# Attention in a two-layer network on one core: maxima placed by VectorE's room, and softmax denominators partly summed on GpSimd

## The reference

```python
q = x @ q_w.T ; k, v = split(x @ kv_w.T)          # 16 query heads, 4 key heads, head size 32
q, k = apply_rope(q), apply_rope(k)
logits = einsum('bhqd,bhkd->bhqk', q, k_ctx) / sqrt(32)
logits = logits + causal_mask
probs = softmax(logits, axis=-1)
out = einsum('bhqk,bhkd->bhqd', probs, v_ctx)
return out @ c_w.T
```

## Time and profile before

| | |
|---|---|
| runs (3) | median 1434.9 us, 1433.83 to 1436.38 |
| profiled execution | 1431.71 us, of which the span of the instructions is 1430.0 us |
| TensorE matmuls (PE) | busy 1348.8 us, 94% of the span |
| VectorE (DVE) | 973.9 us, 68% |
| ScalarE (ACT) | 661.3 us, 46% |
| GpSimd (POOL) | 698.8 us, 49% |
| mean granted clock of TensorE | 0.98 of full speed |
| chain that ended last | PE 65%, DVE 22%, ACT 5%, POOL 3% |

### The profile page before, as it was taken

One profiled execution on the slowest core, in us unless ns is written; L12 is line 12 of the kernel. 1 busy time (PEld: TensorE's weight loads), 2 busy tenths in 40 slices (PEclk: granted clock), 3 DMA queues, 4 the chain that ended last, 5 costly groups with the idle time before them and its releaser, 6 DMA issues.

```text
span 1430.0 us, 19458 instructions
## 1 busy us (share of the span) xinstructions
PE 1348.8 (94%) x7206; PEld 918.9 (64%) x7206; DVE 973.9 (68%) x1959; ACT 661.3 (46%) x1151; POOL 698.8 (49%) x836
## 2 busy tenths in 40 slices
PE   6988999999989899989999999999999999999996
PEld 5875445555455454555554447788888888888885
DVE  5997475755657776676665534577668767886776
ACT  6654233231314554445463574455454645454442
POOL 2676131421313323234243366487678768766863
PEclk9999999999999899999999999999999999999998
DMA  9100110203213111134020411522223232432300
GB/s 336 63 1 1 74 59 16 89 1 96 74 44 97 53 46 49 35 86 143 3 75 10 135 58 60 205 89 89 89 89 147 99 114 98 158 122 88 118 30 29
DMA packets 46270, 116.86 MB, mean 82 GB/s; under 512 B 3420, under 2 KB 4448, under 8 KB 42336
## 3 DMA queue, kind: packets, MB, share of 16 engines
q1 hardware_dynamic: 45104, 114.31, 23.8%
q10 hardware_dynamic: 1072, 1.31, 0.3%
HBM read 92.28 MB, written 23.07 MB: 81 GB/s over the span
## 4 chain that ended last, share of the span: by engine, by line
PE 65%; DVE 22%; ACT 5%; POOL 3%; issue 3%; DMA 1%; SPq 0%; POOLq 0%; DVEq 0%; ACTq 0%
PE PS L1657 63%; DVE cm L626 4%; DVE SM L642 3%; DVE PS L829 2%; DVE SM L638 2%; PE PS L1666 1%; DVE tm L626 1%; ACT EX L1241 1%; DVE hm L635 1%; DVE SM L643 1%; DMA rw<-in_L_ffn_w_up 1%; POOL xA L1472 1%; POOL SM L1472 1%; DVE SM L632 1%; DVE hm L626 1%
## 5 line engine op out<-in xcount | busy, mean ns | idle before, releaser
L1241 ACT ACTIVATE EX<-PS 128x512 f32<-128x512 f32 (+3 forms) x384 | 170.2, 495 | 154.9 <-PE PS L1657 153.9
L1472 POOL TENSOR_TENSOR ws_g<-rw,ws_g 128x512 fp32r<-128x512 f32 x64 | 138.5, 2164 | 124.8 <-ACT ws_g L1062 124.8
L1472 POOL TENSOR_TENSOR SM<-SM 128x1 f32<-128x1 f32 x128 | 82.5, 644 | 233.3 <-DVE SM L632 230.5
L1657 PE MATMUL PS<-KG,QG 96*128 96x512 f32 (+3 forms) x384 | 141.1, 392 | 21.5 <-DVE SM L829 9.0
L1576 POOL TENSOR_SCALAR_AFFINE_SELECT EX<-EX 128x128 f32<-128x128 f32 x256 | 75.3, 303 | 161.7 <-ACT EX L1241 158.3
L829 DVE CUSTOM_DVE_ANT_0 PS<-PS,MW 128x128 f32<-128x128 f32 (+3 forms) x256 | 122.4, 500 | 43.9 <-PE PS L1657 43.3
L1657 PE MATMUL PS<-QG,KG 98*128 98x512 f32 (+3 forms) x384 | 135.6, 382 | 3.2 <-ACT EX L1241 3.0
L1441 ACT ACTIVATE ab<-hm 128x512 f32<-128x512 f32 x64 | 40.5, 633 | 203.6 <-DVE hm L626 203.6
L1657 PE MATMUL PS<-ws_d,HH 128*128 128x512 f32 x528 | 125.7, 389 | 0.7 <-DVE HH L626 0.7
L638 DVE TENSOR_REDUCE SM<-PS 128x1 f32<-128x512 f32 x128 | 87.7, 686 | 55.4 <-PE PS L1657 55.1
L1657 PEld LDWEIGHTS PS<-QG,KG 98*128 98x128 f32 x384 | 72.0, 192 | 76.2 <-issue 45.3
(11 more groups left out here) (204 smaller groups left out, 2798.7 us busy)
## 6 DMA issues: line engine op xcount, KB each, us to landing
rw<-in_L_ffn_w_gate SPq DMA_DIRECT2D x16, 1024.0 KB, 5.1
rw<-in_L_ffn_w_up SPq DMA_DIRECT2D x16, 1024.0 KB, 5.1
rw<-in_L_ffn_w_down SPq DMA_DIRECT2D x16, 1024.0 KB, 6.9
QG<-qs SPq DMA_DIRECT2D x48, 256.0 KB, 4.5
raw<-in_L_ffn_w SPq DMA_DIRECT2D x3, 2816.0 KB, 11.7
qs<-stg SPq DMA_DIRECT2D x16, 512.0 KB, 3.5
xA<-xs SPq DMA_DIRECT2D x2, 2048.0 KB, 8.8
ys<-xA SPq DMA_DIRECT2D x4, 1024.0 KB, 5.9
```

The lines of the kernel that those rows point to most:

```text
L1241: e.activation(EX[:, n % 16, 0:W], PS[:, score_bank(n), 0:W], ACT.Exp, scale=ISQ, bias=0.0).then_inc(S["ex"], 1)
L1472: return e.tensor_tensor(out, a, b, op)
L1657: return e.matmul(out, l, r, start=start, stop=stop, skip_group_check=free)
```

## The change

Three things are changed.

1. **Places of the maxima.** From unit 144 on (group 3 and later), the steady rate of nine per ten chunks with its two bounds is replaced by `room[n]`, a number for what a chunk leaves to VectorE (more for wide scores, projections and units; less for statistics, rotations, the transposes of the denominators), and `effort(x)`, what a maximum takes. Each half of a group has a window of chunks, and its units are spread over it in proportion. The transposes `h` follow where 6000 of room have gone by. Within a chunk the other parts stand ahead of the maxima. With it, unit 10 goes from the chunks 126/130 to 114/118 and unit 11 from 154/158 to 174/178; the copies and subtractions of the output weights CW from 170-182 to 194-206; SP's write of unit 10 from 143 to 132, and its load of the residual rows from 200 to 206.

2. **Sums on GpSimd.** In groups 2 to 6, second half, the exponentials of steps j = 0 to 3 are added up per head into a new tile ES [128, 4, 512] (`add_up`: EX + EX for j = 1, then ES + EX), 12 additions for each group, 60 in all.

3. **Ones products.** For these four steps `weigh` multiplies by ones once, ES at j = 3, where it had multiplied EX at each. New waits: the ones product on the last addition, ScalarE's `exp` on the addition that reads the slot of the ring four steps back.

```diff
+        ES = at("ES", [128, 4, 512], F32, 24)
...
+        def added(t):
+
+            return 2 <= steps3[t][0] <= 6 and steps3[t][1] == 1 and steps3[t][2] < 4
+
+        def esum_at(t, a):
+
+            return 12 * (steps3[t][0] - 2) + 4 * max(0, steps3[t][2] - 1) + a + 1
...
-        for n, y in ((26, 8), (82, 9), (130, 10), (158, 11)):
+        for n, y in ((26, 8), (82, 9), (118, 10), (178, 11)):
...
+        room = []
+        for n in range(NS):
+            r = 120 + 3 * width(n // 4)
+            r += sum({"u": 1200, "V": 1200, "p": 1200, "t3": -600, "VT": 1024}.get(t[0], 0) for t in behind[n])
+            r -= 1700 * (n % 48 in (8, 24)) + 2400 * (n % 48 in (10, 27)) + 5000 * (n in rotate)
+            r -= 1600 * (n + 6 in proj_at) + 2600 * (n - 2 in proj_at) + 2600 * (n in (28, 30, 34, 36))
+            room.append(max(0, r))
...
+        def effort(x):
+            g, f, a, i, k0 = units[x]
+            return 1450 if k0 + 512 <= 128 * i else 300 + 10 * (128 * (i + 1) - k0) // 4
...
+        for x0, x1, n0, n1 in [(48 * g + 16 * f, 48 * g + 16 + 32 * f, max(98, 48 * g - 51 + 14 * f), 48 * g - 37 + 34 * f)
+                               for g in range(3, 8) for f in range(2)]:
+            total, seen, n = sum(effort(x) for x in range(x0, x1)), 0, n0
+            for x in range(x0, x1):
+                while sum(room[n0:n + 1]) * total < seen * sum(room[n0:n1]):
+                    n += 1
+                seen += effort(x)
+                behind[n].append(("m", x))
+            behind[later(n, 6000)].append(("h", x0 // 48 * 2 + x0 % 48 // 16))
...
             def exp(n):
...
+                if n >= 16 and added(n // 4 - 4):
+                    w.wait_ge(S["esum"], esum_at(n // 4 - 4, n % 4))
...
+            def add_up(n):
+
+                t, a = divmod(n, 4)
+                first = steps3[t][2] == 1
+                w.wait_ge(S["ex"], n + 1)
+                if first:
+
+                    w.wait_ge(S["pj"], 20)
+                    w.wait_ge(S["pvd"], t - 9 if t - 9 >= 12 * 2 else 0)
+                else:
+                    w.wait_ge(S["esum"], esum_at(t - 1, a))
+                tt(ES[:, a, :], EX[:, (n - 4) % 16, :] if first else ES[:, a, :], EX[:, n % 16, :], ALU.add).then_inc(
+                    S["esum"], 1)
...
+                if not added(t) or j == 3:
+                    first = 3 if added(t) else 0
+                    if j == first:
+                        w.wait_ge(S["de"], 2 * g + f)
+                    if added(t):
+                        w.wait_ge(S["esum"], esum_at(t, 3))
                     for a in range(4):
-                        last = mm(PS[32 * a:32 * a + 32, bank, q0 - 512 * f:512], left,
-                                  EX[:, (4 * t + a) % 16, 0:width(t)], j == 0, j == 4 * f + 3, free=True)
+                        last = mm(PS[32 * a:32 * a + 32, 7, q0 - 512 * f:512], onesf[:, 0:32],
+                                  ES[:, a, :] if added(t) else EX[:, (4 * t + a) % 16, 0:width(t)],
+                                  j == first, j == 4 * f + 3, free=True)
```

More of the change, by code:

```diff
@@ L45 @@
 pj ue rp qh ql d_w0 d_w1 d_k0 d_k1 d_k2 d_k3 d_q00 d_q01 d_q10 d_q11 vj vt vtp va
-sx mxr nm mtp mth mtl d_m0 d_m1 st ex sel pvd oe de rd oo d_xc cwh cwl
+sx mxr nm mtp mth mtl d_m0 d_m1 st ex sel pvd oe de rd oo esum d_xc cwh cwl
 ehi ot ep pc mv6 rs6 en ey d_ys0 d_ys1
@@ L330, in network, with later @@
             behind[n] += [("p", i, 0), ("p", i, 1)]
-        last = 12
-        for x in range(48, 8 * 48):
-            g, n = divmod(x, 48)
-            last = max(last, 12 + (x - 48) * 9 / 10, 48 * g - 36 + n - 16 if n >= 16 else 0)
-            behind[int(last)].append(("m", x))
-            if n in (15, 47):
-                behind[int(last) + 3].append(("h", 2 * g + n // 32))
+        room = []
[5 more added lines that the diff above has]
+            room.append(max(0, r))
+        def later(n, r):
+            m = n + 1
+            while sum(room[n + 1:m]) < r:
+                m += 1
+            return m
+        def effort(x):
+            g, f, a, i, k0 = units[x]
+            return 1450 if k0 + 512 <= 128 * i else 300 + 10 * (128 * (i + 1) - k0) // 4
+        for x in range(48, 144):
+            last = max(12 + (x - 48) * 9 // 10, x - 52 if x >= 112 else 0)
+            behind[last].append(("m", x))
+            if x % 48 in (15, 47):
+                behind[last + 3].append(("h", x // 48 * 2 + x % 48 // 32))
+        for x0, x1, n0, n1 in [(48 * g + 16 * f, 48 * g + 16 + 32 * f, max(98, 48 * g - 51 + 14 * f), 48 * g - 37 + 34 * f)
[7 more added lines that the diff above has]
+            behind[later(n, 6000)].append(("h", x0 // 48 * 2 + x0 % 48 // 16))
+        for n in range(NS):
+            parts, more = ([t for t in behind[n] if (t[0] == "m") == kind] for kind in (False, True))
+            behind[n] = []
+            for t in parts:
+                behind[n] += [t]
+            behind[n] += more
         tops = bits(first + [t for v in behind for t in v])
@@ L523, in sp_program @@
                         m_in(t[1])
-                if n in (42, 96, 143, 172):
-                    unit_out((42, 96, 143, 172).index(n) + 8)
+                if n in (42, 96, 132, 172):
+                    unit_out((42, 96, 132, 172).index(n) + 8)
                 if n in (100, 112, 156, 202):
@@ L530, in sp_program @@
                     k_in(4 + g)
-                if n == 200:
+                if n == 206:
                     written(10)
@@ L1309, in attention @@
                         drain(2 * (n // 48) - 1)
-                    if n in (170, 174, 178, 182):
-                        c = (n - 170) // 4
+                    if n in (194, 198, 202, 206):
+                        c = (n - 194) // 4
                         w.wait_ge(S["d_xs1"], 16)
@@ L1571, in attention @@
                         scale(2 * (n // 48))
+                    if added(n // 4) and steps3[n // 4][2] > 0:
+                        add_up(n)
                     if diagonal(n // 4):
@@ L1863, in weigh @@
                 w.wait_ge(S["va"], 3 if g < 4 else 4)
-                for bank, left, drained in ((6, VG[g // 4][:, j, g % 4 * 32:(g % 4 + 1) * 32], "oe"),
-                                            (7, onesf[:, 0:32], "de")):
-                    if j == 0:
-                        w.wait_ge(S[drained], 2 * g + f)
+                if j == 0:
+                    w.wait_ge(S["oe"], 2 * g + f)
+                for a in range(4):
+                    last = mm(PS[32 * a:32 * a + 32, 6, q0 - 512 * f:512], VG[g // 4][:, j, g % 4 * 32:(g % 4 + 1) * 32],
+                              EX[:, (4 * t + a) % 16, 0:width(t)], j == 0, j == 4 * f + 3, free=True)
+                if not added(t) or j == 3:
[4 more added lines that the diff above has]
+                        w.wait_ge(S["esum"], esum_at(t, 3))
                     for a in range(4):
-                        last = mm(PS[32 * a:32 * a + 32, bank, q0 - 512 * f:512], left,
-                                  EX[:, (4 * t + a) % 16, 0:width(t)], j == 0, j == 4 * f + 3, free=True)
+                        last = mm(PS[32 * a:32 * a + 32, 7, q0 - 512 * f:512], onesf[:, 0:32],
+                                  ES[:, a, :] if added(t) else EX[:, (4 * t + a) % 16, 0:width(t)],
+                                  j == first, j == 4 * f + 3, free=True)
                 last.then_inc(S["pvd"], 1)
```

## The result

The changed kernel takes 1444.6 us (median), the kernel before 1436.4 beside it: ratio 1.0048, 95% interval 1.0029 to 1.0068. It is **slower by about 7 us** by the ratio, where 13 less were forecast.

The account below looks back on a forecast made before the run. It took TensorE to lose 38 us in groups 2 to 7, largely waiting for VectorE's crowded maxima and at lower clock. Maxima 15.3 us saved, additions with ones products 2.2 lost: 13.1 off the median, 1422 us, range 1405 to 1437.

Parts of the forecast that it names:

- The maxima: Attention from chunk 98 on: spreading the maxima by room saves 19.2 us, less 3.9 that come back, net 15.3.
- what comes back: First eight chunks of groups: thicker maxima cost 0.5 us in four groups, 1.7 in group 2, 3.9 with the queue's start.
- Bursts: Chunks 187, 235, 283: crowded maxima cost 11.2 us, lower clock 3.5; with 4.5 at unit 10's rotation, 19.2 go.
- Rival (c): Maxima gain little: crowds move to the group starts with lower clock behind; 4 us left of 15.3, 1433; chance 0.10.
- So nothing is late: SP's queue: unit 11's write at 172 waits for GpSimd's last subtraction (chunk 190), reads due at 192; cost put at nothing.
- The 4.5 us of its rotation: Chunks 130 and 134: TensorE's wait at unit 10's rotation and the slow step after it go, 4.5 us saved.
- Ones products: Groups 2 to 6, second half: 15 times four matmuls dropped at 0.88 us each, 13.2 us saved where TensorE is the bound.
- Additions: 60 on GpSimd at 1.25 us each; with waits, clock and hold-ups against the 13.2 us saved, a loss of 2.2.
- rival (b): GpSimd becomes the bound: additions take 1.56 us, chains 3.7 us longer each, result slower at 1444; chance 0.12.
- The waits: For GpSimd: TensorE 3.5 us in group 6, 2.0 in 2; ScalarE 1.6 in 4, 2.8 in 5; 9.9 in all.
- the hold-up in group 2: Unit 10's rotations (chunks 122, 126) beside additions: six VectorE operations held by GpSimd, put at 2.0 us.
- The sign for (c): VectorE releasing TensorE in the first eight chunks of every group for more than 2 us.

Follow-up runs that it names:

- e2_places: The changed kernel without its additions, ones products at every step as before, new places kept: 1438.2 us, ratio 1.0020 to the kernel before.
- g2_flat: New places, no additions, unit 11's write at chunk 193, first-half maxima windows of 20 chunks instead of 14, group 2's from chunk 102: 1425.4 us, ratio 0.9947.
- f3_write_late: New places, no additions, SP's write of unit 11 at chunk 193 instead of 172, behind the read of group 5's queries: 1435.5 us, ratio 0.9988.
- f4_no_ones: New places, no additions, ones products of j = 0, 1, 2 left out in second halves of groups 2 to 6: 1429.8 us, ratio 0.9953.
- f1_late: The changed kernel with the sum ES multiplied by ones two steps later, behind the products of j = 5: 1444.9 us, ratio 1.0055.
- f2_late_old: The additions with the same later product of ES, but maxima, units and weights at their old rate and places: 1444.7 us, ratio 1.0054.
- e1_after: The changed kernel run again, unaltered, for a profile at the usual clock: 1444.4 us, ratio 1.0044 to the kernel before.

## Why the prediction was wrong

**The maxima: the step that failed.** 15.3 us saved were forecast, +0.2% measured (2.9 us slower by the ratio, 5.0 by the groups). The term that failed is "what comes back", put at 3.9 us, and with it the moves of units 10 and 11, put at nothing. The pieces, as time over TensorE's work priced as in the prediction, before and in e2_places:

- *Bursts.* In the last eight chunks of groups 2 to 5, where the three bursts and unit 10's old rotation lay, the excess fell from 23.7 to 2.2 us: 21.5, where 19.2 had been put. This was right. (The burst at chunk 283 has 16 maxima in the trace, not 17, which changes its excess by 0.2.)
- *Given back at the starts.* 3.9 us forecast; the excess of the first eight chunks of groups 2 to 6 rose from 2.0 to 15.2, **13.2**. The step compared VectorE's sum with TensorE's sum over eight chunks (6.5 against 6.0) and took the difference. But the two don't fill a stretch evenly: the starts of groups 3 and 4 take 8.0 us with VectorE busy for 6.6 and 6.8. That the three banks between them are the reason is argued; no run has another number of banks. And the half clock, charged to the bursts, was not charged to the crowd that replaced them: 10.2 us of it in the first eight chunks of group 2, 17.8 in the whole group. g2_flat shows that this is the part that can be had back (7.8 us, in group 2). Rival (c) had this mechanism, at 10% and with 4 us left of the 15.3.
- *Unit 11.* "So nothing is late" was wrong: the excess of chunks 200 to 207 rose by **4.2** us, and f3_write_late gets 4.6 back. The text had listed the reads due at 192 behind the waiting write, but took the subtraction's place in the program (chunk 190) for its time. In e2_places it ends at 670.07 and the read starts at 671.38; in f3_write_late, where everything stands 1.9 us later, it starts at 668.39, which is 666.5 there: 4.9 us earlier.
- *Unit 10.* The 4.5 us of its rotation were counted as saved; in e2_places the chunks 128 to 135 have **3.7** us over their work, 3.4 us of them at half clock. It moved with the unit.

These four pieces cancel: 21.5 gained, 21.1 given back. The groups 2 to 7 of e2_places are 5.0 us longer than before, so that some 5 us more lie spread over the other stretches. The chunks 104 to 111 have 4.2 us at half clock; the rest stays open.

**Ones products.** 13.2 us, 0.88 each, where TensorE is the bound. In groups 3 and 6 of f4_no_ones the full price was seen (2.6 us each); over all, it has 9.1 by the groups, and 5 or 9.6 by the ratios, as the one or the other kernel is taken beside it.

**Additions.** The price of one was right: 1.28 us in the median and 1.25 from start to start when undisturbed. So rival (b) is not what happened, and that the measured 1444.6 is its 1444 is chance: only beside unit 10's rotation in group 2 did seven additions take 1.56 us apiece, and of the 20 us by which the forecast missed 18 are there in e2_places, without any addition. The waits were there and mostly shorter: in group 6 2.6 us where 3.5 was put, in groups 4 and 5 ScalarE waits 1.75 and 1.00 us where 1.6 and 2.8 were put. The whole part was put at a loss of 2.2 us and is one of 2.8 by the groups and 3.4 by the ratios: nearly right, with its terms off in both directions. What was too small is the hold-up in group 2, put at 2.0 us: its six operations take 4.84 + 4.35 instead of 6 x 0.69, 5.05 more. By the rule of the Trainium skill (SBUF — State Buffer, section "SBUF: two separate sides") the prediction had an estimate of 5.2; the trace has these 5.05. Missing from the sum: VectorE's OT operations (2.37 us for 0.68) and the selects, for which TensorE waits 2.41 us in group 6 of f1_late, where the later product gained nothing.

**The signs named beforehand** came half. There was no stretch of maxima alone near the old bursts, and the clock was at its upper level there. The ones product of j = 3 was released by GpSimd in group 6, though in group 2 VectorE's wait hid it, and group 6 was not shorter. Group 4 was 1.5 us longer and group 5 3.6 shorter, where 5 to 9 less were named. The sign for (c) was not met as put: TensorE's idle time in the first eight chunks of a group is some 1 us, not 2; the loss shows in the distances from start to start and in the clock, and the sign should have been put on those.

## What to carry to other kernels

When a burst of work for a second engine is spread, price the clock that falls behind the new crowd as that behind the old: of what g2_flat gained nearly all was in the one group whose clock had fallen. Judge by whole groups and not by the crowded stretch, since a shorter start can be given back behind it. Try the window's width: 14 and 20 chunks gave 0.9988 and 0.9947 without additions, 20 and 24 gave 0.9929 and 0.9944 with them, a difference within the intervals. A queue's wait is placed by the time at which its releaser runs, not by its place in the program. Here work on an idle engine was free only where its whole queue, and what shares its access to SBUF, had that time: 24 additions in the wrong two groups cost 6 us (3.8 by the groups), while 12 in the right one gained the full 2.6 us by the groups of the products that they replaced.

## What the runs showed of the hardware that was not expected

A VectorE operation with both inputs in SBUF was held by several GpSimd instructions in a row: 128 x 16, 0.18 us in most places, took 3.42 beside an addition and twelve selects in f1_late, and 4.80 beside subtractions and selects in f2_late_old. The effect runs both ways, with additions of up to 1.74 us for 1.25. The maxima, read from PSUM, kept their 0.69 in the median (0.73 at most). Before the clock fell in group 2 TensorE had waited for VectorE for 0.28 and 0.24 us, no longer, and it then stayed at the lower level for 13.6 us (e1_after, from 565.8). And identical code behind attention took 577 to 584 us from one execution to the next; the cause stays open.
